# Logits of the next pair but one, two block steps earlier in the second step of a two-step graph attention kernel

## The chip, the cores and the metric

The kernel runs on one core of one Trainium2 chip. The metric is the device time of one execution in microseconds (us). Every duration below comes from one profiled execution of the kernel before, or from the three times shown beside it.

The core has five engines with instruction queues of their own: PE (TensorE, matrix multiplication and transposes), ACT (ScalarE), DVE (VectorE), POOL (GpSimd) and SP (SyncE, which here only issues DMAs). PEld is PE's loading of weights. Each engine works through its queue in order and waits on semaphores that the others raise.

## What is computed

`x` has 3327 rows of 128 numbers and `adj` is 3327 x 3327. Two steps run one after the other; in each, a dense matrix R is applied to one copy of the features and a sparse attention matrix A to the other.

```python
q = X @ W1.T @ W2.T
k = X @ W3.T
logits = q @ k.T / TAU
probs = jax.nn.softmax(logits, axis=-1)
idx = jnp.argsort(-probs, axis=-1)
sp = jnp.take_along_axis(probs, idx, axis=-1)
cs = jnp.cumsum(sp, axis=-1)
keep_sorted = cs - sp < TOP_P                  # TOP_P = 0.9
A = probs * mask                               # mask: the kept ones
A = A / jnp.maximum(A.sum(-1, keepdims=True), 1e-12)
...
R = S + jnp.eye(N); R = R / R.sum(-1, keepdims=True)
for n in range(2):
    A = _top_p_attention(Xa, W1, W2, W3)
    Xf = R @ Xf
    Xa = A @ Xa
    Z = Z + Xf @ U1[n].T + Xa @ U2[n].T
h = X + Z
# layer norm of h with ln_g, ln_b, then layer norm of (x + that)
```

## The kernel before

**Tiles and pairs.** The rows are cut into NT = 26 tiles of 128 (padded to 3328), and two tiles make a pair, so there are NPAIR = 13 pairs, numbered 0 to 12. A row of 3328 columns is cut into NCH = 7 chunks: six of 512 columns and a last one of 256 (255 real ones for logits).

**Units, blocks and bodies.** A unit is the product of one 128-row tile of a matrix with the features: an A unit takes the tile of the attention matrix, an R unit the tile of R. Each unit is seven blocks, one for each chunk. For a block PE transposes four 128 x 128 pieces into a PSUM bank (L602), ACT copies the bank to `blkT` (L721), and two steps later PE multiplies the four pieces with the features (L623). The last chunk has two pieces instead of four. Units are grouped in bodies. In step two, body p holds the two A units of pair p (blocks 0 to 13) and then `STEP_R[p]` R units, four and three in turn (blocks 14 to 41 or 14 to 34). Body p therefore has two steps more than blocks. In step i PE issues, in this order: the transposes of block i, the logits of a chunk if the table `emit` has an entry for i, and the multiplication of block i - 2. ACT issues in step i: the copy of block i, the two copies of a logits chunk if `emit` has an entry, the storing of a finished unit's sums (`part_h`, L742, or `new_x`, L738), parts of the layer norm, and exponentials if the table `exps` has an entry. The last transposes of the A units are in step 13; the sums of the second A unit are stored in step 15.

**Logits.** `logits(s, p, c)` is two matmuls, one for each tile of pair p, with 64 contracted rows (L554). `store_logits` copies both results from PSUM into `E` (L674). `E01` has two areas, and in step two pairs p and p + 2 share one. From body 0 of step two on, there is one PSUM bank for each tile of the pair (bank 0 and bank 1), so that the matmuls of one chunk wait until ACT has copied the chunk before. The lines that set this are:

```python
before = q - (1 if q >= late_logits else 2)          # L545
pe.wait_ge(logits_done, 2 * before + xx + 1)         # L551
if c == 0 and free_at[s, p]:                         # L670, ACT
    act.wait_ge(blk_ready, free_at[s, p])
```

`free_at` is the end of the transposes of the second A unit of pair p - 2, in the same area.

**What a pair needs.** In body p of step two the logits of pair p + 2 are made. DVE takes the eight largest of each run of 32 logits (`v.max`, MAX8, L841), finds the row maximum (`negm`, L866), and ACT makes the exponentials of the pair in step 36 of body p, or steps 36 to 41 where the body has four R units (L691 for the candidates, L696 for the rows). DVE then searches for the threshold of the pair (`search`, from L937 on) and settles it (L1232 to L1261: MATCH_REPLACE8 and the masking), which lets the transposes of that pair's A units start. In its iteration for pair p, DVE searches pair p, takes the maxima of pair p + 1 from some 21 us into the search on (`link.fill = 3`, three MAX8 behind each linked instruction), and then settles pair p. Some pairs also go through `level`, a finer search over the whole rows.

**R tiles.** Two buffers `S` hold two tiles of adj. SP issues the load of R unit n once the transposes of R unit n - 2 are done (L393), and POOL adds the identity (L451) after its work on the sums and the layer norm, in the order of the units; the R unit's first transposes wait for that.

Of the kernel before, what the change touches and what calls it, by code (L numbers as in the profile page):

```python
# [6 lines left out]
def gnn_top_p_kernel(nc, x, adj, W1, W2, W3, U1, U2, ln_g, ln_b, out):  # L7
# [16 lines left out]
    NCH = (NT + CH - 1) // CH  # L24
# [57 lines left out]
    def add_unit(b, kind, s, t):  # L82
        u = Unit()
        u.kind, u.s, u.t, u.k = kind, s, t, len(units)
        u.pair, u.x = t // 2, t % 2
        u.ring, u.accs = (2, ("6",)) if b.early else (3, ("3", "6"))
        if kind == "R":
            u.n, u.src = len(r_units), len(r_units) % 2
            r_units.append(u)
        u.turned = s == 0  # L90
        if u.turned:
            u.j = len(t_units)
            t_units.append(u)
        else:
            u.m = len(units) - len(t_units)
        u.acc = u.accs[u.k % len(u.accs)]
        u.acc_before = acc_user.get(u.acc, -1)
        acc_user[u.acc] = u.k
        u.first = len(seq_unit)
        for c in range(NCH):  # L100
            i = len(seq_unit)
            slot = len(b.seqs) % u.ring
            seq_unit.append(u)
            seq_chunk.append(c)
            seq_slot.append(slot)
            seq_before.append(slot_user.get(slot, -1))
            slot_user[slot] = i
            b.seqs.append(i)
        u.end = len(seq_unit)
        units.append(u)  # L110
        b.units.append(u)

    def new_body(early, s, p, off):
        b = Body()
        b.early, b.s, b.p, b.off = early, s, p, off
        b.units, b.seqs, b.emit, b.exps, b.turn, b.mul, b.first_exps, b.late = [], [], {}, {}, {}, {}, [], {}
        b.look = 1 if early else 2
        bodies.append(b)
        return b

    b = new_body(True, 0, -1, 0)
# [7 lines left out]
    for p in range(NPAIR):  # L129
        more = p + 2 < NPAIR  # L130
        b = new_body(True, 0, p, 0)
# [15 lines left out]
    b = new_body(False, 1, -1, 0)  # L147
# [8 lines left out]
    for p in range(NPAIR):  # L156
        b = new_body(False, 1, p, 0)
        for xx in range(2):
            add_unit(b, "A", 1, 2 * p + xx)
        for n in range(STEP_R[p]):  # L160
            m = len(r_units)
            add_unit(b, "R", m // NT, m % NT)
        if p + 2 < NPAIR:
            for c in range(NCH):
                b.emit[2 * NCH + 2 + c] = (1, p + 2, c)

            for k in range(6):
                b.exps.setdefault(5 * NCH + 1 + (k if STEP_R[p] > 3 else 0), []).append((1, p + 2, k))
# [1207 lines left out]
```

## Time and profile before

| | us |
|---|---|
| three runs | 1434.26, 1433.92, 1429.52 |
| median of the three | 1433.92 |
| profiled execution, its own time | 1431.37 |
| span of its instructions | 1429.3 |
| DVE busy | 1281.5 (90%) |
| PE busy | 1228.1 (86%) |
| ACT busy | 930.7 (65%) |
| POOL busy | 340.5 (24%) |

The time of an execution is its span and some 2.1 us around it. Times in the rows are us from the span's start. Step two's bodies begin at about 525 us (body 0) and the last ends at about 1415 us. The busy shares are means over stages that have different limits, so they don't tell which engine sets the end; the chain of the work that ended last does. In the timeline, one row is a run of like instructions: its start, its length, the engine, the line, and, in brackets, how long the engine sat idle before it and what released it.

### The profile page before, as it was taken

The numbers are of one execution on the slowest core, as the hardware profiler recorded it, in microseconds if no ns is written. First come the engines' busy times: TensorE is split into PE (matmuls) and PEld (weight loads), VectorE is DVE, ScalarE is ACT, GpSimd is POOL, SyncE is SP. The second block draws the span as 40 slices with busy tenths as digits, with TensorE's granted clock in tenths as the row PEclk, the third lists the DMA queues.
The fourth block names the chain that finished last, engine by engine and source line by source line (L and its number), as shares of the span: only waits on it lengthen the run. The fifth ranks groups of instructions, "written<-read, shape, count | busy, mean of one in ns | idle before, by whom it ended". The sixth has DMA issues, their size and how long they took to land.

```text
span 1429.3 us, 29789 instructions
## 1 busy us (share of the span) xinstructions
PE 1228.1 (86%) x9162; PEld 1036.5 (73%) x9162; DVE 1281.5 (90%) x7010; ACT 930.7 (65%) x2026; POOL 340.5 (24%) x584
## 2 busy tenths in 40 slices
PE   7999999999997979897989796919895885929896
PEld 3677777777785968887888786818784775828796
DVE  5998989998976888899989989999998999999995
ACT  5888887788757565756575555636764746646764
POOL 0112322232201331312141220202332222212242
PEclk9999999999998989998999898969998897969998
DMA  5000000000021541412132132211312041211421
GB/s 205 2 1 2 2 2 2 2 2 2 2 97 49 193 145 38 156 49 97 55 139 96 50 103 91 97 48 49 145 50 96 2 145 49 94 52 50 145 49 49
DMA packets 16599, 96.49 MB, mean 68 GB/s; under 512 B 1251, under 2 KB 8930, under 8 KB 9730
## 3 DMA queue, kind: packets, MB, share of 16 engines
q1 hardware_dynamic: 16384, 94.14, 18.7%
q8 instruction: 72, 1.18, 0.3%
q14 instruction: 143, 1.17, 0.3%
HBM read 92.43 MB, written 1.70 MB: 66 GB/s over the span
## 4 chain that ended last, share of the span: by engine, by line
PE 44%; DVE 37%; ACT 11%; issue 5%; POOL 1%; DVEq 1%; DMA 0%; SPq 0%; ACTq 0%; POOLq 0%
PE bank L623 24%; DVE cand L841 13%; PE bank L602 11%; DVE junkC L898 8%; PE bank L554 5%; ACT E L696 4%; DVE E L1241 2%; ACT blkT L721 2%; ACT cand L691 2%; DVE sub L1064 2%; DVE E L1261 1%; PE bank L638 1%; DVE junkS L898 1%; DVE slots L963 1%; ACT S L696 1%
## 5 line engine op out<-in xcount | busy, mean ns | idle before, releaser
L721 ACT ACTIVATE blkT<-bank 128x512 f32<-128x512 f32 (+1 forms) x728 | 406.4, 565 | 284.7 <-PE bank L602 280.7
L841 DVE MAX8 cand<-E 128x8 f32<-128x32 f32 (+1 forms) x2992 | 404.2, 192 | 41.8 <-ACT E L674 26.4
L623 PEld LDWEIGHTS bank<-X,blkT 128*128 128x128 f32 x2704 | 329.1, 191 | 104.1 <-ACT blkT L721 71.8
L623 PE MATMUL bank<-X,blkT 128*128 128x129 f32 (+1 forms) x2704 | 375.9, 281 | 10.3 <-ACT blkT L721 9.1
L602 PE MATMUL bank<-ident,S 128*128 128x128 f32 x1560 | 242.0, 275 | 17.4 <-POOL S L451 15.6
L602 PE MATMUL bank<-ident,E 128*128 128x128 f32 x1144 | 183.0, 285 | 81.0 <-DVE E L1261 81.0
L898 DVE SCALAR_TENSOR_TENSOR junkC<-cand,st 128x128 f32<-128x128 f32 (+2 forms) x390 | 236.0, 613 | 2.0
L623 PE MATMUL bank<-YF,blkT 128*128 128x128 f32 x1352 | 192.7, 287 | 36.1 <-ACT blkT L721 36.1
L623 PEld LDWEIGHTS bank<-YF,blkT 128*128 128x128 f32 x1352 | 171.6, 199 | 68.7 <-ACT blkT L721 57.6
L554 PE MATMUL bank<-kT,Q 64*128 64x512 f32 (+1 forms) x728 | 197.0, 613 | 8.7 <-ACT E L674 8.4
L602 PEld LDWEIGHTS bank<-ident,E 128*128 128x128 f32 x1144 | 143.7, 148 | 83.3 <-DVE E L1261 82.1
L602 PEld LDWEIGHTS bank<-ident,S 128*128 128x128 f32 x1560 | 186.2, 142 | 22.4 <-POOL S L451 17.7
L674 ACT ACTIVATE E<-bank 128x512 f32<-128x512 f32 (+1 forms) x308 | 157.9, 567 | 55.8 <-PE bank L554 55.2
L623 PE MATMUL bank<-YA,blkT 128*128 128x128 f32 x1352 | 187.0, 282 | 0.5 <-ACT blkT L721 0.5
L623 PEld LDWEIGHTS bank<-YA,blkT 128*128 128x128 f32 x1352 | 171.9, 198 | 1.0 <-ACT part_h L742 0.7
L1261 DVE SCALAR_TENSOR_TENSOR E<-E,st 128x3328 f32<-128x3328 f32 x42 | 155.6, 3721 | 8.8 <-DVE flag_i L1041 6.9
L696 ACT ACTIVATE E<-E,negm 128x1664 f32<-128x1664 f32 x88 | 147.4, 1677 | 0.0
L691 ACT ACTIVATE cand<-cand,negm 128x312 f32<-128x312 f32 (+2 forms) x104 | 55.5, 540 | 81.5 <-DVE negm L866 81.5
L480 POOL TENSOR_TENSOR H<-hy,H 128x128 f32<-128x128 f32 x26 | 39.0, 1500 | 281.0 <-ACT hy L757 281.0
L1241 DVE MATCH_REPLACE8 E<-gone,E 128x832 f32<-128x832 f32 x104 | 103.8, 1009 | 0.0
L554 PEld LDWEIGHTS bank<-kT,Q 64*128 64x128 f32 x728 | 56.6, 185 | 43.3 <-issue 27.2
L487 POOL TENSOR_TENSOR H<-part_h,H 128x128 f32<-128x128 f32 x50 | 31.0, 620 | 195.7 <-ACT part_h L742 195.5
(226 smaller groups left out, 1336.6 us busy)
## 6 DMA issues: line engine op xcount, KB each, us to landing
S<-in_adj_dram SPq DMA_DIRECT2D x50, 1663.5 KB, 6.8
S<-in_adj_dram SPq DMA_DIRECT2D x2, 1455.6 KB, 8.5
X<-in_x_dram SPq DMA_DIRECT2D x6, 256.0 KB, 5.4
out_dram<-H SPq DMA_DIRECT2D x1, 1408.0 KB
S<-in_adj_dram SPq DMA_DIRECT2D x2, 194.9 KB, 9.7
u_in<-in_L_gnn_U_dram SPq DMA_DIRECT2D x4, 64.0 KB, 9.6
out_dram<-H SPq DMA_DIRECT2D x1, 128.0 KB
w_in<-in_L_gnn_W_dram SPq DMA_DIRECT2D x2, 32.0 KB, 2.1
```

The lines of the kernel that those rows point to most:

```text
L480: pool.tensor_tensor(H[:, u.t, :], hy[:, z, 0:D], H[:, u.t, :], ALU.add)
L554: pe.matmul(lg_banks(q)[xx][:, 0:LW[c]], Q[h0:h1, p, :], kT[h0:h1, s, c * BANK:c * BANK + LW[c]], start=True, stop=True).then_inc(logits_r ...
L602: m = pe.transpose(BLK[early][slot][:, b * P:(b + 1) * P], src[:, j * P:(j + 1) * P], ident[:, :])
L623: m = pe.matmul(bank[int(u.acc)][:, 0:width], blkT[:, slot, b * P:(b + 1) * P], rhs[:, j, 0:width], start=(j == 0), stop=(j == NT - 1))
L674: act.activation(E[where_e[s, p]][:, xx, c * BANK:c * BANK + LW[c]], lg_banks(q)[xx][:, 0:LW[c]], ACT.Copy).then_inc(logits_done, 1)
L691: act.activation(c, c, ACT.Exp, bias=negm[:, par, xx:xx + 1], scale=1.0, accum_out=total[:, par, xx:xx + 1])
L696: return act.activation(e[:, xx, lo:hi], e[:, xx, lo:hi], ACT.Exp, bias=negm[:, par, xx:xx + 1], scale=1.0, accum_out=Zh[:, par, xx, half: ...
L721: act.activation(blkT[:, slot, 0:w], BLK[early][slot][:, 0:w], ACT.Copy).then_inc(blk_done, 1)
L841: v.max(cand[:, par, xx, 8 * r:8 * r + 8], E[where_e[self.s, self.p]][:, xx, r * w:min((r + 1) * w, N)]).then_inc(s_max, 1)
L898: return v.scalar_tensor_tensor(out=out, in0=a, scalar=limit, in1=a, op0=ALU.is_lt, op1=ALU.mult, accum_out=total)
L1241: link.post(v.match_replace(back, gone[:, xx, k, :], back, 0.0))
L1261: v.scalar_tensor_tensor(out=e[:, xx, :], in0=e[:, xx, :], scalar=one(TSTAR, xx), in1=e[:, xx, :], op0=ALU.is_ge, op1=ALU.mult, accum_out= ...
```

## The change

The seven chunks of the logits of pair p + 2 are issued in steps 14 to 20 of body p in place of steps 16 to 22. That holds for the eleven bodies 0 to 10 of step two, on PE and on ACT. The exponentials stay in step 36. Step one, DVE, POOL and SP have the same instructions in the same order.

```diff
         if p + 2 < NPAIR:
             for c in range(NCH):
-                b.emit[2 * NCH + 2 + c] = (1, p + 2, c)
+                b.emit[2 * NCH + c] = (1, p + 2, c)
 
             for k in range(6):
                 b.exps.setdefault(5 * NCH + 1 + (k if STEP_R[p] > 3 else 0), []).append((1, p + 2, k))
```

PE in body 4, steps 14 to 16, before. The transposes of `S` are those of the first R unit, the multiplications with `YA` the last two of the second A unit, and `kT,Q` are the logits of pair 6:

```order
L602 MATMUL bank5<-ident,S 128x128 x4
L623 MATMUL bank6<-YA,blkT 128x128 x4
L602 MATMUL bank2<-ident,S 128x128 x4
L623 MATMUL bank6<-YA,blkT 128x128 x2
L602 MATMUL bank4<-ident,S 128x128 x4
L554 MATMUL bank0<-kT,Q 128x512
L554 MATMUL bank1<-kT,Q 128x512
L623 MATMUL bank3<-X0,blkT 128x129 x4
```

And in the changed kernel, the same steps:

```order
L602 MATMUL bank5<-ident,S 128x128 x4
L554 MATMUL bank0<-kT,Q 128x512
L554 MATMUL bank1<-kT,Q 128x512
L623 MATMUL bank6<-YA,blkT 128x128 x4
L602 MATMUL bank2<-ident,S 128x128 x4
L554 MATMUL bank0<-kT,Q 128x512
L554 MATMUL bank1<-kT,Q 128x512
L623 MATMUL bank6<-YA,blkT 128x128 x2
L602 MATMUL bank4<-ident,S 128x128 x4
L554 MATMUL bank0<-kT,Q 128x512
L554 MATMUL bank1<-kT,Q 128x512
L623 MATMUL bank3<-X0,blkT 128x129 x4
```

Two chunks of logits have moved ahead, and between the second and the third there now stands the short multiplication (two pieces, `x2`) of the A unit's last block. Before, it stood between transposes alone.

ACT in body 4, steps 14 to 16, before:

```order
L721 ACTIVATE blkT<-bank5 128x512
L721 ACTIVATE blkT<-bank2 128x512
L742 ACTIVATE part_h<-bank6,a_inv 128x128
L721 ACTIVATE blkT<-bank4 128x512
L674 ACTIVATE E01<-bank0 128x512
L674 ACTIVATE E01<-bank1 128x512
```

And in the changed kernel:

```order
L721 ACTIVATE blkT<-bank5 128x512
L674 ACTIVATE E01<-bank0 128x512
L674 ACTIVATE E01<-bank1 128x512
L721 ACTIVATE blkT<-bank2 128x512
L674 ACTIVATE E01<-bank0 128x512
L674 ACTIVATE E01<-bank1 128x512
L742 ACTIVATE part_h<-bank6,a_inv 128x128
L721 ACTIVATE blkT<-bank4 128x512
L674 ACTIVATE E01<-bank0 128x512
L674 ACTIVATE E01<-bank1 128x512
```

The copies of the logits have moved with their matmuls, and the storing of the second A unit's sums now stands between two chunks' copies.

## Rows read from the trace of the kernel before

**Rows 1.** Part 1 of the page: busy time, share of span, instructions.

```profile
PE 1228.1 (86%) x9162; PEld 1036.5 (73%) x9162; DVE 1281.5 (90%) x7010; ACT 930.7 (65%) x2026; POOL 340.5 (24%) x584
```

**Rows 2.** The chain that ended last, merged: start us, length us, engine, tile, line.

```profile
797.32 5.19 ACT E L696 x7
...
823.85 1.11 PE bank L554 x4
844.80 2.52 DVE cand L841 x26
...
1034.94 1.33 ACT E L696
...
1282.00 2.82 PE bank L602 x12
```

**Rows 3.** Waits of DVE from 500 us on: us in total, times, longest.

```profile
DVE st L937 <- ACT E L696: 9.6, 5, 3.7
...
DVE cand L841 <- ACT E L674: 8.1, 5, 2.9
```

**Rows 4.** Timeline of DVE: its first maxima in the iterations of pairs 1 and 5.

```profile
558.66 0.38 DVE L841 MAX8 cand<-E 128x8 f32<-128x32 f32 x3 [2.88 <-ACT E L674]
...
825.63 0.38 DVE L841 MAX8 cand<-E 128x8 f32<-128x32 f32 x3 [2.10 <-ACT E L674]
```

**Rows 5.** Timelines: `negm` on DVE and first exponentials on ACT, bodies 0, 3, 4.

```profile
584.79 0.17 DVE L866 TENSOR_SCALAR negm<-negm 128x2 f32<-128x2 f32 x1
592.11 0.55 ACT L691 ACTIVATE cand<-cand,negm 128x312 f32<-128x312 f32 x1
...
785.83 0.17 DVE L866 TENSOR_SCALAR negm<-negm 128x2 f32<-128x2 f32 x1
792.28 0.55 ACT L691 ACTIVATE cand<-cand,negm 128x312 f32<-128x312 f32 x1
...
869.50 0.55 ACT L691 ACTIVATE cand<-cand,negm 128x312 f32<-128x312 f32 x1 [9.36 <-DVE negm L866]
```

**Rows 6.** Timeline of PE in body 4, steps 14 to 20 (x8 for four pieces).

```profile
821.04 0.60 PE L602 MATMUL bank<-ident,S 128*128 128x128 f32 x4
...
822.80 0.61 PE L623 MATMUL bank<-YA,blkT 128*128 128x128 f32 x4
823.25 0.60 PE L602 MATMUL bank<-ident,S 128*128 128x128 f32 x4
823.78 1.13 PE L554 MATMUL bank<-kT,Q 64*128 64x512 f32 x4
824.84 1.16 PE L623 MATMUL bank<-X,blkT 128*128 128x129 f32 x8
...
826.37 1.13 PE L554 MATMUL bank<-kT,Q 64*128 64x512 f32 x4
...
831.54 1.13 PE L554 MATMUL bank<-kT,Q 64*128 64x512 f32 x4
...
833.90 1.13 PE L554 MATMUL bank<-kT,Q 64*128 64x512 f32 x4
```

**Rows 7.** Timeline of ACT in body 4: copies of the first and the fourth chunk.

```profile
825.00 1.09 ACT L674 ACTIVATE E<-bank 128x512 f32<-128x512 f32 x2 [0.52 <-PE bank L554]
...
832.70 1.08 ACT L674 ACTIVATE E<-bank 128x512 f32<-128x512 f32 x2 [0.46 <-PE bank L554]
```

**Rows 8.** SP and POOL in body 4, third R tile; then the page's DMA row.

```profile
834.00 0.35 SPq L393 DMA_DIRECT2D S<-in_adj_dram  x1
...
845.91 0.46 POOL L451 TENSOR_TENSOR S<-S,ident 128x128 f32<-128x128 f32 x1
...
S<-in_adj_dram SPq DMA_DIRECT2D x50, 1663.5 KB, 6.8
```

**Rows 9.** Busy time by stretch: start:end, length, PE, PEld, DVE, ACT, POOL, PEclk, DMA.

```profile
534.80:555.00 20.20, 19.43 (x147) 19.14 (x148) 19.22 (x73) 8.88 (x19) 3.15 (x4) 0.83 0.00 1
...
738.60:790.20 51.60, 51.39 (x409) 44.87 (x410) 50.19 (x362) 29.96 (x60) 12.23 (x26) 1.00 0.20 73
```

## The prediction

> **What bounds the kernel now.** I read the page's busy times first. DVE at 90% and PE at 86% [rows 1] are both too high for one of them to be the bound everywhere, so the order of the chain is what counts. The chain that ended last [rows 2] is to be read by where it changes engines. Up to 823.85 us step two's chain runs through PE's blocks and ACT's exponentials (such as the piece at 797.32). At 823.85 it passes through two logits matmuls of body 4 and goes over to DVE (844.80), where it stays for most of the next 450 us. It leaves DVE twice: for body 6, whose exponentials end at 1036.3 (the piece at 1034.94), and for good at 1282.00, where PE starts body 10 and PE and ACT set the rest.
>
> So an edit that brings logits forward pays only where DVE both waits for logits and is itself on the chain. DVE's waits [rows 3] give the most that this can be: 8.1 us in 5 waits of DVE for the copies of logits, in all of step two. Two of them are in the timeline [rows 4]: 2.88 us before 558.66, and 2.10 us before 825.63. The other three are 3.1 us together, all before body 4.
>
> Of these, only the one before 825.63 is on the chain. The exponentials of a pair stay in step 36, and ACT reaches that step late: in body 0 `negm` is there at 584.79 + 0.17 = 584.96 and the first exponential starts at 592.11, which is 7.2 us of slack; in body 3 it is 792.28 - 786.00 = 6.3 us [rows 5]. There ACT doesn't wait for DVE, and maxima that come 2 us earlier make the slack longer and nothing else. In body 4 it is the other way round: ACT sat idle for 9.36 us until `negm` came, and its exponentials start at 869.50. What DVE gains before that, everything behind it gains.
>
> **The change part by part.** No instruction is added or taken away. Two chunks of logits stand two steps further up in each of 11 bodies.
>
> *How much earlier the first logits come.* PE's rows of body 4 [rows 6] are to be read as a clockwork. Step 14 begins at 821.04 and step 16 at 823.25, and logits start 823.78 - 823.25 = 0.53 behind the transposes. In the changed kernel they start at 821.04 + 0.53 = 821.57, so 2.21 us earlier than at 823.78. DVE was ready at 825.63 - 2.10 = 823.53. The first copy now ends in time for DVE to go on at 825.63 - 2.21 = 823.42. The wait of 2.10 goes entirely, though by only 0.1 us. Chunks then follow each other at 2.59 us (826.37 - 823.78), and DVE needs about 3 us for the 32 MAX8 of a chunk even without the search's own instructions: its chain piece of 26 takes 2.52 us [rows 2]. So no new wait for a later chunk appears. **Gain: 2.10 us.** What is late next at that point is DVE's own search. I let the gain travel to the end, since from there to 1282 the chain is DVE's, and body 6 itself starts when DVE has settled its pair.
>
> *What the new place costs PE.* The matmuls of one chunk wait until ACT has copied the chunk before. In the fourth pair of matmuls this can be seen closely: they start at 831.54 [rows 6], ACT's copies run from 832.70 to 833.78 [rows 7], and the next ones start at 833.90, 2.36 us after the last and 0.12 behind the copies, in the step whose transposes are two pieces instead of four. I take 2.36 us as the shortest period that the copies allow. In the changed kernel the short multiplication of the A unit's last block stands between the second and the third chunk. It takes 0.45 us (823.25 - 822.80). PE would be ready again after 1.06 (824.84 - 823.78) + 0.45 + 0.53 = 2.04 us, and up to 0.1 later if the short multiplication loses as much behind logits as the long one does. It then waits for 2.36 - 2.04 = 0.32 at most, and 2.36 - 2.14 = 0.22 at least. I take 0.23 us, near the low end, because the long multiplication behind logits is indeed 0.1 longer. A lower bound of nothing is also possible, were the 2.36 PE's own time; an upper bound is 0.32 + 0.37, one store of sums more on ACT, were ACT the late one. Before, this short multiplication had no logits around it, and the last chunk of logits (255 columns) had no successor to wait, so nothing is given back.
>
> This cost counts in the bodies that are on the chain: 0 to 3 in front of 823.85, then 6 and 10. 6 x 0.23 = **1.4 us lost** (0 to 4.1 by the bounds). In the other five bodies PE has idle time to cover it.
>
> *The third R tile.* The load of the R tile for step 28 is issued when the transposes of step 20 are through, at 834.00 in body 4. Six chunks of logits instead of four now precede them, which moves the issue by 2 x (2.59 - 1.33) + 0.23 = 2.75 us (a step without logits takes 1.33: steps 14 and 15 take 2.21, and the short multiplication in them saves 0.45, so (2.21 + 0.45) / 2). The load takes 6.8 us, so it lands at 834.00 + 2.75 + 6.8 = 843.6. POOL takes that tile at 845.91 [rows 8], behind its own work. The load stays hidden by 2.3 us, and costs nothing; without that cover, each us of it would be a us of PE in that body. DVE, POOL and SP pass no new instruction, and the norm's work on ACT and POOL in steps 18 and 25 stands in the same steps as the R tiles that wait for it.
>
> *The area in `E`.* The copies need the end of the A unit's transposes, step 13, and ACT's own block copy of step 14 comes behind that. The edit is at the earliest place that needs no new wait.
>
> **Sum.** -2.10 + 1.4 = -0.7 us. Against the profiled execution, 1431.37, that is 1430.7; against the median of the runs, 1433.92, it is 1433.2. The four executions have a mean of 1432.3, and less 0.7 that is 1431.6. I forecast **1432.0 us**, no change that can be measured. About 0.5%, 7 us, is what a measurement of this kernel can tell from none.
>
> One rule of the Trainium skill speaks against the change (Perfetto Trace Analysis, Optimizing Tensor Performance, Matmuls): independent groups of matmuls should rotate through PSUM banks, so that the emptying of one overlaps the next. The logits here have one bank per tile, and the 2.36 us period agrees with the rule; by it the crowded place is the short multiplication, and the sum holds it already.
>
> **Rivals.**
>
> *All of DVE's waits count* (chance 0.04). Then 8.1 us less what the earlier start can give: 1431.4 - 8.1 = 1423 us. It would need DVE to be the bound in bodies 0 to 3. The 6.3 and 7.2 us of slack before the exponentials [rows 5] speak against it.
>
> *PE loses more than DVE gains* (chance 0.15). The place is step 16 of bodies 0 to 3, 6 and 10, the price the upper bound above, 0.69 us each: 4.1 - 2.1 = +2.0, so 1434 us, slower, but not measurably. It decides from 0.35 us per body on. For it speaks that ACT has the sums' store as well between the second and the third chunk; against it, that ACT is idle for 0.46 us before the copies of a chunk [rows 7].
>
> *The granted clock falls in the denser steps* (chance 0.03). In the stretch 534.8 to 555.0 the granted clock is 0.83, that is, (1 - 0.83) / 0.5 x 20.2 = 6.9 us at 1.2 GHz and the rest at 2.4 GHz, right behind a stretch in which PE stood waiting for ACT [rows 9]. Another such piece in each of six bodies would cost 6 x 6.9 / 2 = 21 us: 1452 us. Against it: in body 3, with seven chunks of logits in the same tight alternation, the clock was 1.00 throughout. By the Trainium skill (TensorE: Matmul & The Clock Gate, A second HAM failure mode: psum-queue depth-cycling), frequent short idling between groups that cycle through PSUM can drop the clock; body 3 doesn't bear that out.
>
> *The logits don't come earlier at all* (chance 0.03), because something that I read as free holds ACT: only the cost is left, 1431.4 + 1.4 = 1432.8.
>
> **How the numbers follow.** Forecast 0.75, rivals 0.04, 0.15, 0.03, 0.03. The likeliest case gives 1432.0. The low end is the lowest execution shown less the whole gain, 1429.5 - 2.1 = 1427.4; the high end the highest plus the second rival's loss, 1434.3 + 2.0 = 1436.3. That holds all but the first and third rival, and some of what executions scatter. Faster by over 0.5%: 0.04, the first rival. Slower by over 0.5%: 0.04, the third and a little scatter. The rest, 0.92, is within 0.5%.
>
> **What would show it.** Right: DVE's wait before its first maxima of pair 6 is gone, and so are most of those of pairs 2 and 4; the slack before the exponentials in bodies 0 and 3 grows by about 2 us; from the end of the exponentials in body 3 (797.32 + 5.19 = 802.5 on the chain) to the exponentials of body 4 (869.50) it takes 65 us in place of 67; PE's third logits of a body start 2.36 us behind the second. Wrong: exponentials in bodies 0 to 3 that start before their old time relative to the body, which would make DVE the bound there; a wait of PE for POOL or a DMA at step 28 that is longer than before; a clock below 1.00 in bodies 1 or 3.

## The result

| | us | runs |
|---|---|---|
| before, median | 1431.68 | 9 (1428.89 to 1434.26) |
| changed, median | 1438.26 | 9 (1435.09 to 1441.62) |
| profiled execution before, span | 1429.3 | |
| profiled execution changed, span | 1435.0 | |

The changed kernel is slower: the ratio is 1.0046, with a 95% interval of 1.0033 to 1.006, that is 6.6 us. The forecast was 1432.0 us with a range of 1427.4 to 1436.3. The time lies outside the range, and what was to be no measurable change is a small loss, of 4.7 to 8.6 us by the interval. Here and below, the ratio is an estimate over all the runs with an interval of its own; it isn't exactly the quotient of the two medians.

### The profile page after: what moved, and what is told of

Same layout as the page of the kernel before. It is cut to its first block, busy times and chain, and to the rows that moved or that the text cites. A ratio compares the mean times of both kernels' runs of the same rounds, so it can differ in the third digit from the quotient of the medians.

```text
span 1435.0 us, 29789 instructions
## 1 busy us (share of the span) xinstructions
PE 1230.9 (86%) x9162; PEld 1039.0 (72%) x9162; DVE 1280.8 (89%) x7010; ACT 929.1 (65%) x2026; POOL 353.3 (25%) x584
## 4 chain that ended last, share of the span: by engine, by line
DVE 42%; PE 39%; ACT 10%; issue 6%; POOL 2%; DVEq 1%; DMA 0%; SPq 0%; ACTq 0%; POOLq 0%
PE bank L623 21%; DVE cand L841 15%; PE bank L602 10%; DVE junkC L898 9%; PE bank L554 5%; ACT E L696 4%; DVE E L1241 3%; ACT blkT L721 2%; ACT cand L691 2%; DVE E L1261 2%; DVE sub L1064 2%; DVE slots L963 1%; PE bank L638 1%; DVE st L908 1%; DVE junkS L898 1%
## 5 line engine op out<-in xcount | busy, mean ns | idle before, releaser
L1261 DVE SCALAR_TENSOR_TENSOR E<-E,st 128x3328 f32<-128x3328 f32 x42 | 156.0, 3730 | 8.8 <-DVE flag_i L1041 6.9
```

Source lines behind the costliest of these rows:

```text
L1261: v.scalar_tensor_tensor(out=e[:, xx, :], in0=e[:, xx, :], scalar=one(TSTAR, xx), in1=e[:, xx, :], op0=ALU.is_ge, op1=ALU.mult, accum_out= ...
```

## The profile after

Part 1 of the changed kernel's page, to be read against [rows 1]:

```profile
PE 1230.9 (86%) x9162; PEld 1039.0 (72%) x9162; DVE 1280.8 (89%) x7010; ACT 929.1 (65%) x2026; POOL 353.3 (25%) x584
```

PE, DVE and ACT have the busy time that they had, within 3 us. POOL has the same 584 instructions and is busy for 353.3 us; before it was 340.5. Nothing in the edit touches POOL, so some of its instructions must have become longer. The chain that ended last shows where, as against [rows 2]:

```profile
587.34 3.81 POOL S L451
...
722.73 4.03 POOL YF L477
...
848.86 3.63 DVE cand L841 x38
```

Two single POOL instructions of about 4 us each are now on the chain, one in body 0 and one in body 2. Before, no piece of POOL stood on it between the start of body 0 and body 4. These two account for 6.8 of POOL's 12.8 us more; most of the rest are two small instructions, L464 and L463, which take 3.58 and 3.36 us at 595.01 and 730.77, and for which nobody waits. The timelines of POOL, DVE and PE around the first of them, in the changed kernel:

```profile
586.74 0.60 POOL L477 TENSOR_SCALAR YF<-hy,row_inv 128x128 f32<-128x128 f32 x1
587.30 3.83 POOL L451 TENSOR_TENSOR S<-S,ident 128x128 f32<-128x128 f32 x1
...
587.14 3.69 DVE L1261 SCALAR_TENSOR_TENSOR E<-E,st 128x3328 f32<-128x3328 f32 x1
...
591.19 0.66 PE L602 MATMUL bank<-ident,S 128*128 128x128 f32 x4 [2.40 <-POOL S L451]
```

and the same place before:

```profile
588.14 0.46 POOL L451 TENSOR_TENSOR S<-S,ident 128x128 f32<-128x128 f32 x1
...
588.42 0.08 DVE L1241 MATCH_VALUE_LOAD E<-gone,E 128x8 f32 x1
588.49 1.01 DVE L1241 MATCH_REPLACE8 E<-gone,E 128x832 f32<-128x832 f32 x1
...
589.53 3.68 DVE L1261 SCALAR_TENSOR_TENSOR E<-E,st 128x3328 f32<-128x3328 f32 x1
...
589.46 0.60 PE L602 MATMUL bank<-ident,S 128*128 128x128 f32 x4
```

Before, POOL adds the identity for the R tile of step 35 in 0.46 us, beside DVE's MATCH_REPLACE8, and DVE's masking (L1261) starts 0.9 us behind it. Now the masking starts 2.4 us earlier, just ahead of POOL's instruction. POOL's 0.46 us become 3.83 us, and it ends 0.3 us behind the masking: 587.30 + 3.83 = 591.13 against 587.14 + 3.69 = 590.83. PE stands still for 2.40 us. In body 2 it is L477, the instruction ahead of the addition, that is met; it takes 4.05 us in place of 0.60. PE waits as long there:

```profile
722.71 4.05 POOL L477 TENSOR_SCALAR YF<-hy,row_inv 128x128 f32<-128x128 f32 x1
...
722.68 3.69 DVE L1261 SCALAR_TENSOR_TENSOR E<-E,st 128x3328 f32<-128x3328 f32 x1
...
727.23 0.66 PE L602 MATMUL bank<-ident,S 128*128 128x128 f32 x4 [2.47 <-POOL S L451]
```

The wait that DVE has lost comes back as a wait of DVE for ACT's exponentials, as against [rows 3]:

```profile
DVE st L937 <- ACT E L696: 20.5, 5, 8.4
DVE cand L841 <- issue: 8.9, 3, 4.5
```

The five waits for the copies of logits (8.1 us) are gone altogether. The waits for exponentials went from 9.6 to 20.5 us; behind bodies 0 and 2 they are 7.9 and 8.4 us in place of 3.7 and 3.5, and there ACT is late by PE's wait as well.

Why bodies 0 and 2 and not 1 and 3? The waits for logits that the change takes away were not alike. [Rows 4] show those of bodies 0 and 4, 2.88 and 2.10 us. The ones of bodies 1 and 2, before:

```profile
626.08 0.38 DVE L841 MAX8 cand<-E 128x8 f32<-128x32 f32 x3 [0.18 <-ACT E L674]
...
692.52 0.38 DVE L841 MAX8 cand<-E 128x8 f32<-128x32 f32 x3 [2.74 <-ACT E L674]
```

In bodies 1 and 3 DVE waited for logits for 0.18 and 0.19 us only, so its later instructions hardly moved there.

The other rows of the prediction have their answers too. PE's clockwork in body 4, as against [rows 6]:

```profile
825.87 1.13 PE L554 MATMUL bank<-kT,Q 64*128 64x512 f32 x4
...
828.45 1.13 PE L554 MATMUL bank<-kT,Q 64*128 64x512 f32 x4
...
830.59 1.28 PE L554 MATMUL bank<-kT,Q 64*128 64x512 f32 x4
...
833.33 1.13 PE L554 MATMUL bank<-kT,Q 64*128 64x512 f32 x4
```

The third chunk's matmuls start 2.14 us behind the second's and the fourth's 2.74 behind those, 4.88 in all. The delay is seen inside the third chunk, whose matmuls take 1.28 us in place of 1.13; the profile doesn't name what held them. Without it the distance would be some 2.13 + 2.59 = 4.72 (2.13 is the prediction's 2.04 and most of the 0.1 it allowed), so PE loses 0.16 us per body. ACT's copies of the second chunk:

```profile
829.61 1.09 ACT L674 ACTIVATE E<-bank 128x512 f32<-128x512 f32 x2 [0.46 <-PE bank L554]
```

They end at 829.61 + 1.09 = 830.70, and the third chunk's matmuls have started at 830.59: the tile that goes first has a bank of its own, and needs only the first of the two copies.

Then DVE's maxima behind a branch in the iteration of pair 5, as the timeline of DVE has them: before, then changed, with SP's issue of the load of adj in the changed kernel between them:

```profile
844.80 0.29 DVE L841 MAX8 cand<-E 128x8 f32<-128x32 f32 x2 [1.72 <-issue]
```

```profile
840.97 0.35 SPq L393 DMA_DIRECT2D S<-in_adj_dram  x1
...
848.86 0.29 DVE L841 MAX8 cand<-E 128x8 f32<-128x32 f32 x2 [3.41 <-issue]
```

This is a wait for nothing that the profile shows, right behind a branch. It grew by 1.7 us. The load of adj was issued at 834.00 before [rows 8], 9.1 us ahead of the start of this wait; now it is issued 4.5 us ahead of it and is under way when DVE comes to the branch, as a load takes 6.8 us.

## The experiments

The theory after this reading is **A**: the early logits free DVE, its masking moves onto POOL's work for the R tile of step 35 in bodies 0 and 2, and PE waits. The rivals are **B**, the matmuls of the logits wait for ACT's copies, and **C**, the loss lies behind body 4. All times stand beside runs of the kernel before on the same chip. The diffs are against the kernel before, unless it is said otherwise.

### Only bodies 0 and 2, and all but these

```diff
-                b.emit[2 * NCH + 2 + c] = (1, p + 2, c)
+                b.emit[2 * NCH + (0 if p in (0, 2) else 2) + c] = (1, p + 2, c)
```

> Only bodies 0 and 2 of step two have their logits two steps earlier. Theory A (collision): DVE, freed of its wait for logits, starts the masking instruction L1261 (3.7 us, two operands from SBUF) some 2.4 us earlier, onto POOL's addition of the identity for the R tile of step 35; POOL's instruction then lasts 3.8 us in place of 0.46 and PE waits 2.4 us for it. Two bodies: 2 x (2.4 + 0.16) = 5.1 us slower than before, with a wait of PE for L451 of about 2.4 us at step 35 of bodies 0 and 2. Theory B (the matmuls of the logits wait for ACT, 0.16 us per body as the changed kernel's trace has it): +0.3 us. Theory C (the loss comes from behind body 4: code loading and body 10): +0.3 us.

Measured: 1439.81 us against 1431.16, ratio 1.0052 (1.0038 to 1.0065).

```diff
-                b.emit[2 * NCH + 2 + c] = (1, p + 2, c)
+                b.emit[2 * NCH + (0 if p not in (0, 2) else 2) + c] = (1, p + 2, c)
```

> All bodies but 0 and 2 have their logits two steps earlier. Theory A: what is left of the changed kernel's +6.6 us without the two collisions, so +1 to +2 us over before. Theory B: +5 us (9 of 11 bodies). Theory C: +6 us.

Measured: 1431.11 us against 1431.16, ratio 0.9998 (0.9988 to 1.0007).

The whole loss sits in two of the eleven bodies. B and C fall as its cause: on the second kernel they had put +5 and +6 us, and it is at -0.3 us (-1.7 to +1.0). Theory A has the place right, but neither of its sums: it had +1 to +2 us for the second kernel, and the first lost 7.4 us (5.4 to 9.3), more than the 5.1 us that I had added up. The first kernel's timeline of body 0, POOL and PE, and the busy time of a stretch behind it:

```profile
588.59 4.05 POOL L477 TENSOR_SCALAR YF<-hy,row_inv 128x128 f32<-128x128 f32 x1
...
593.12 0.71 PE L602 MATMUL bank<-ident,S 128*128 128x128 f32 x4 [2.47 <-POOL S L451]
```

```profile
594.00:598.00 4.00, 4.00 (x25) 4.00 (x24) 3.96 (x6) 1.76 (x5) 0.35 (x1) 0.62 0.37 155
```

Right behind the wait the granted clock over 4 us is 0.62, so most of that stretch ran at 1.2 GHz: (1 - 0.62) / 0.5 x 4 = 3.0 us of it, of which half, 1.5 us, is lost. In the changed kernel's own trace the granted clock was 1.00 behind both waits (590 to 594 and 727 to 731 us). Three profiled executions, the changed kernel's, this one and that of the early logits with POOL's new order (further down), have six of these waits at step 35 of bodies 0 and 2. Two were followed by such a fall, this one and the one of body 2 in the last of the three (0.58 over 727.8 to 731.8 us). So a collision costs 2.2 to 2.5 us and, in some executions, some 1.5 us more. By the Trainium skill (TensorE: Matmul & The Clock Gate, Part 1: The HAM clock gate) the clock falls when PE has been idle; that agrees with this row, though not every wait of this length brought it about.

### DVE held back, everything else as changed

In the changed kernel (against which this diff is), DVE's first maxima in the iterations of pairs 1 and 3 wait for the second chunk of logits in place of the first:

```diff
-                            dve.wait_ge(logits_done, 2 * lg_seq(self.s, self.p, c) + xx + 1)
+                            first = 1 if self.n == 0 and self.s and self.p in (2, 4) else 0
+                            dve.wait_ge(logits_done, 2 * lg_seq(self.s, self.p, c + first) + xx + 1)
```

> The changed kernel, but in the iterations of pairs 1 and 3 DVE waits for the second chunk of the next pair's logits before its first maximum, which puts its maxima and the masking behind them back to about where they stood before (0.7 us earlier at most). PE, ACT and POOL have the changed kernel's order. Theory A: POOL's L451 for step 35 of bodies 0 and 2 lasts 0.46 us again, PE doesn't wait for it, and the kernel is 4.8 us faster than the changed one, so +1 to +2 us over before. Theories B and C: as slow as the changed kernel, +6.6 us, since PE's order is what it was there.

Measured: 1432.57 us against 1431.16, ratio 1.0003 (0.9993 to 1.0013). A wait was added to the busiest engine and the kernel became some 6 us faster than the changed one, where 4.8 were expected. POOL and DVE in body 0:

```profile
589.32 0.46 POOL L451 TENSOR_TENSOR S<-S,ident 128x128 f32<-128x128 f32 x1
...
591.41 3.68 DVE L1262 SCALAR_TENSOR_TENSOR E<-E,st 128x3328 f32<-128x3328 f32 x1
```

The addition takes 0.46 us again, and PE doesn't wait for it. PE's order is that of the changed kernel, so B falls a second time.

### The masking in four pieces

The changed kernel again (the diff is against it), with L1261 cut in the iterations of pairs 1 and 3; the sums of the pieces are added behind it:

```diff
+                            if s and p in (1, 3):
+                                for k in range(MATCH):
+                                    piece = e[:, xx, k * MW:(k + 1) * MW]
+                                    ins = v.scalar_tensor_tensor(out=piece, in0=piece, scalar=one(TSTAR, xx), in1=piece,
+                                                                 op0=ALU.is_ge, op1=ALU.mult, accum_out=part[:, xx, k:k + 1])
...
```

> The changed kernel, but in the iterations of pairs 1 and 3 the masking L1261 is four instructions of 832 columns (about 0.95 us each) in place of one of 3328. Theory A in the form that POOL's instruction waits for the end of the DVE instruction that it meets: POOL's L451 lasts at most 1.4 us, PE's wait at step 35 falls below 0.5 us, and the kernel is about 4 us faster than the changed one (+2 to +3 over before). If POOL is kept out for the whole of the masking, however it is cut, the wait stays at 2.4 us and the time at +6.6 us.

Measured: 1432.90 us against 1431.16, ratio 1.0008 (0.9999 to 1.0018). POOL, DVE and PE in body 0:

```profile
587.89 1.43 POOL L477 TENSOR_SCALAR YF<-hy,row_inv 128x128 f32<-128x128 f32 x1
589.29 0.98 POOL L451 TENSOR_TENSOR S<-S,ident 128x128 f32<-128x128 f32 x1
...
587.76 1.08 DVE L1264 SCALAR_TENSOR_TENSOR E<-E,st 128x832 f32<-128x832 f32 x1
588.77 1.18 DVE L1264 SCALAR_TENSOR_TENSOR E<-E,st 128x832 f32<-128x832 f32 x1
...
590.33 0.66 PE L602 MATMUL bank<-ident,S 128*128 128x128 f32 x4 [0.39 <-POOL S L451]
```

The overlap is still there, at the same moment, but POOL gets its turn when a piece ends: 1.43 and 0.98 us in place of 4.05 or 3.83, and PE waits 0.39 us. So POOL waits for the end of the DVE instruction that it meets, not for the end of the masking. Only body 0 of this trace tests that. In body 2 POOL's addition had begun 0.23 us before the first piece, and it wasn't held up:

```profile
722.43 0.46 POOL L451 TENSOR_TENSOR S<-S,ident 128x128 f32<-128x128 f32 x1
...
722.66 1.12 DVE L1264 SCALAR_TENSOR_TENSOR E<-E,st 128x832 f32<-128x832 f32 x1
```

### One step earlier in place of two

```diff
-                b.emit[2 * NCH + 2 + c] = (1, p + 2, c)
+                b.emit[2 * NCH + 1 + c] = (1, p + 2, c)
```

> All logits one step earlier, steps 15 to 21. Before, DVE's masking L1261 begins some 0.95 us behind the end of POOL's L451 for step 35 of body 0. Step 15 is 0.88 us long, so DVE's wait shrinks by 0.88, and PE and POOL come 0.16 later: the two then begin within 0.1 us of each other. If the addition is met, L451 lasts 3.8 us in one or both of bodies 0 and 2, in some executions at least, and the time is up to 5 us over before; if it just escapes, the time is that of before within 1 us. The theory doesn't tell which; it tells that no third value comes, and that the time goes with that row.

Measured: 1429.84 us against 1431.24, ratio 0.9998 (0.9986 to 1.0011).

```profile
587.90 0.46 POOL L451 TENSOR_TENSOR S<-S,ident 128x128 f32<-128x128 f32 x1
...
588.75 3.69 DVE L1261 SCALAR_TENSOR_TENSOR E<-E,st 128x3328 f32<-128x3328 f32 x1
```

The masking comes 0.4 us behind the end of the addition, not onto it, and the time is that of before. My figure of 0.1 us for the distance was off, but the time went with the row as said. One step is clear of the collision here and two aren't.

### Only body 4, and the same with a short load

```diff
-                b.emit[2 * NCH + 2 + c] = (1, p + 2, c)
+                b.emit[2 * NCH + (0 if p == 4 else 2) + c] = (1, p + 2, c)
```

> Only body 4 of step two has its logits two steps earlier: the one place where DVE's wait for logits (2.10 us) is on the chain. If the gain were all that happens there, 2.1 us faster than before. By the trace of the changed kernel, the load of the third R tile, now 2.75 us later, meets the loading of DVE's code behind its branch, and DVE's wait after the branch grows from 1.7 to 3.4 us; then 1 us at most is left, no difference that can be measured. No wait of PE for POOL at step 35 of bodies 0 and 2.

Measured: 1432.05 us against 1432.55, ratio 0.9998 (0.9988 to 1.0007).

On top of this, one load is cut short. The kernel then leaves out most of one tile of R, so it only serves to measure:

```diff
+                elif u.n == 26:
+                    sp.dma_start(S[0:16, u.src, 0:N], adj[r0:r0 + 16, :]).then_inc(adj_loaded[u.src], 16)
```

> As only_4, but the adj load of R unit 26 (for step 28 of body 4) brings 16 rows in place of 128; the other rows of that buffer keep an older tile, so that part of R is left out. If the load is what delays DVE's code, DVE's wait before its maxima after the branch in the iteration of pair 5 is 1.7 us or less instead of 3 or more, and the time is 1 to 2 us below only_4. If the code's lateness has another cause, the wait stays above 2.8 us.

Measured: 1428.80 us against 1432.55, ratio 0.9982 (0.997 to 0.9995). The wait behind the branch, first in the kernel with body 4 alone, then with the short load:

```profile
844.61 3.76 DVE L841 MAX8 cand<-E 128x8 f32<-128x32 f32 x38 [3.23 <-issue]
```

```profile
842.90 3.63 DVE L843 MAX8 cand<-E 128x8 f32<-128x32 f32 x38 [1.72 <-issue]
```

With the load cut from 128 rows to 16 the wait is 1.72 us, exactly that of before, and the gain forecast for this place appears: 2.6 us by the ratio (0.7 to 4.3), where the forecast had 2.1. The place itself shows it more closely. From the end of body 3's exponentials (802.5 us in both) to the first of body 4 it takes 64.8 us with the short load, against 67.0 before [rows 5]:

```profile
867.37 0.55 ACT L693 ACTIVATE cand<-cand,negm 128x312 f32<-128x312 f32 x1 [7.91 <-DVE negm L868]
```

With the full load 1.5 of the 2.1 us are lost behind the branch. The other traces agree at this place. Where the load was issued 7.3 to 9.1 us ahead of the wait (before, bodies 0 and 2 alone, one step earlier, and POOL's new order with the logits as before) the wait was 1.71 or 1.72 us; in the seven with the full load issued 4.5 to 5.0 us ahead of it, it was 2.85 to 3.41 us. That DVE's code is what comes late is an inference: in the trace, packets of the kind "instruction" lie there (three of one queue in the 8 us around it, before and with body 4 alone), and the profile names no releaser.

### POOL's addition ahead of its norm work

This one was made to beat both kernels. PE's waits for L451 at steps 28 and 35 of bodies 6 and 10, on the chain, were there before the change. POOL reaches the addition only behind the round of the layer norm, which itself waits for ACT. Here it adds the identity first:

```diff
                 elif u.k <= last_part.k:
                     add_part(u)
+                    next_diagonal(units[u.k + 1])
                     for job in norm_rounds.get(u.k + 1, ()):
                         norm_round(*job)
```

`next_diagonal` is the two `add_diagonal` conditions that stood at the head of the loop, where it is called too, each done once.

> Logits as before. POOL adds the identity to the R tile of the next unit but one before its part of the layer norm, not behind it. If PE's waits for L451 at steps 21, 28 and 35 are POOL's order alone, they go: in bodies 6 and 10, which are on the chain, 1.2 + 2.0 us each, and 1.7 in body 11, of which the tile's load may keep 1.6. 5 to 7 us faster than before. If the loads set those waits, no difference.

Measured: 1428.31 us against 1432.55, ratio 0.9972 (0.9958 to 0.9985). That is 4.0 us faster (2.1 to 6.0), a little less than the 5 to 7 expected. PE's waits for POOL's addition in step two, first before, then with POOL's new order:

```profile
PE bank L602 <- POOL S L451: 15.6, 11, 2.8
```

```profile
PE bank L611 <- POOL S L451: 2.8, 3, 1.4
```

Of the 12.8 us that PE waits less, those in the two bodies on the chain count: from the first transposes of one body to those of the next, body 6 takes 70.3 us in place of 72.7 and body 10 takes 70.1 in place of 71.8, 4.1 us together.

> pool_first with the changed kernel's logits, two steps earlier in all bodies. The collisions of bodies 0 and 2 are between POOL's saving of sums (L475 to L477, L451) and DVE's masking, which this order of POOL doesn't touch: there the identity is added behind the saving as before. So PE's waits of some 2.4 us at step 35 of bodies 0 and 2 stay, and the kernel is 5 us or more slower than pool_first. If putting POOL's addition first cured the collision too, it would be equal to pool_first.

Measured: 1434.34 us against 1432.55, ratio 1.001 (0.9999 to 1.0021), 6.0 us slower than its twin with the logits in their old place by the medians, 5.4 by the ratios. POOL and PE in body 0:

```profile
588.18 3.87 POOL L451 TENSOR_TENSOR S<-S,ident 128x128 f32<-128x128 f32 x1
...
592.11 0.66 PE L611 MATMUL bank<-ident,S 128*128 128x128 f32 x4 [2.44 <-POOL S L451]
```

The collision costs as much in another surrounding, within the noise, which is the comparison of before and changed made a second time.

> POOL's addition ahead of its norm work, as in pool_first, and the logits two steps earlier in all bodies but 0 and 2. With the logits moved but not in 0 and 2 the time was that of before, so this should be equal to pool_first: 1428 us, no difference between the two. Faster than pool_first by 1 us or more would mean that the early logits gain something once PE doesn't wait for POOL.

Measured: 1426.27 us against 1431.24, ratio 0.9969 (0.9958 to 0.9979). It is the fastest kernel here by its ratio, but it can't be told from `pool_first` (0.9972): as expected, the early logits of the other bodies bring nothing that can be measured.

## Why the prediction was wrong, point by point

**What bounds the kernel, and where the gain is: right.** Only DVE's wait before 825.63 was on the chain, and it went entirely. With the load out of the way the gain was seen at that size, 2.2 us in the trace and 2.6 (0.7 to 4.3) in the time.

**"Maxima that come 2 us earlier make the slack longer and nothing else": this step failed**, and the forecast with it. The sum has no term for a wait of PE for POOL; it put that at nothing. The slack before the exponentials did grow: in body 0 from 7.2 to 11.3 us, part of it because PE and ACT came later. In body 3, for which about 2 us were forecast too, it grew by 0.4 us only, since DVE had hardly waited for logits there. But slack only says that nobody waits for the result. Where DVE's instructions then lie in time changes too, and here a 3.7 us instruction moved onto a 0.46 us instruction of POOL that PE does wait for. Two collisions at 2.4 us are 4.9 us, with PE's 0.16 us for each 5.1. That lies within the interval of the 6.6 us. The rest of the 6.6 fits the fall of the clock behind some of these waits; how often it comes in the runs without a profile isn't known. In bodies 1 and 3 nothing was met: from the end of one body's exponentials to the end of the next's they took 64.07 and 64.06 us in place of 63.90 and 63.92, which is the 0.16 us of the crowded step and nothing more. The prediction had named a longer wait of PE for POOL as a sign of being wrong, but at step 28; it came at step 35.

**"DVE, POOL and SP pass no new instruction": true and not enough.** I checked the order on each queue and the waits on semaphores. The meeting of two engines is neither. By the Trainium skill (GPSIMD Engine Reference, Specifications) POOL shares its SBUF interfaces with DVE, and they contend when the DVE instruction has two inputs from SBUF. The traces agree: L451 lasts 3.83 us beside L1261, whose two tensor operands are both `E`. Beside MATCH_REPLACE8 it lasts 0.46 us; that row names `gone` and `E`, but in front of it stands a MATCH_VALUE_LOAD of 8 numbers for the first. No run has the masking with one operand, so that the second operand is what matters rests on the page. The trace of before held the warning, just ahead of body 0. There the same addition takes 3.59 us beside L1261:

```profile
521.54 3.59 POOL L451 TENSOR_TENSOR S<-S,ident 128x128 f32<-128x128 f32 x1
...
521.07 3.75 DVE L1261 SCALAR_TENSOR_TENSOR E<-E,st 128x3328 f32<-128x3328 f32 x1
```

I weighed other rules in its place.

**"I let the gain travel to the end": too simple.** In the changed kernel 1.7 of the 2.1 us were gone 20 us later, behind DVE's branch, since the load of adj moved as well. The prediction had moved that load by 2.75 us, about rightly (2.6 measured from the end of body 3's exponentials), and asked only whether POOL would wait for it. Who else uses the DMA engines in the new place was not asked.

**PE's cost for the crowded step: near in size, by luck.** 0.23 us forecast, 0.16 measured, per body. But 2.36 us is not the shortest period that the copies allow: the third chunk started 2.14 us behind the second, where 2.36 was named as the sign of being right, and ahead of the end of both copies. What makes up the 0.16 us inside the chunk isn't shown.

**The rivals.** The second had the right sign, with the wrong place and price: its own step cost the 0.16 us. The first and the fourth didn't come. The third, the clock, came as a consequence of PE's new wait, not of the denser steps: in the changed kernel's trace the granted clock was 1.00 through bodies 1 and 3 (605 to 656.6 and 742 to 795 us).

**What the two traces can't be used for.** Their spans differ by 5.7 us, close to the 6.6, but partly for other reasons. Body 0, by the ends of the exponentials, is only 1.3 us longer in the changed kernel's: behind its start the granted clock is 0.91 over 20.2 us, where it was 0.83 before [rows 9], and that gives back (0.91 - 0.83) / 0.5 x 20.2 / 2 = 1.6 us. Body 10 took 74.7 us from its first transposes to those of body 11, against 71.8 before. It also took 74.8 us in the kernel with all bodies but 0 and 2, whose time is that of before, and 72.3 with DVE held back, where it has the early logits too. Most of it is the clock. In both traces PE waits 2.01 us for POOL's addition at step 35 of body 10; the 5 us behind that, before and changed:

```profile
1337.60:1342.60 5.00, 4.97 (x45) 4.97 (x46) 4.86 (x15) 3.54 (x10) 0.46 (x1) 1.00 0.57 238
```

```profile
1341.10:1346.10 5.00, 5.00 (x31) 5.00 (x32) 4.90 (x11) 1.95 (x6) 0.41 (x1) 0.66 0.56 235
```

That is (1 - 0.66) / 0.5 x 5 / 2 = 1.7 us. In the first 6 us of the body the granted clock is 0.52 in place of 0.69, another 1.0 us. Together they are 2.7 of the 2.9 us.

**Open.** What decides whether the clock falls behind such a wait, since the same wait of 2.01 us was followed by 1.00 in one trace and by 0.66 in the other.

## What to carry to other kernels

An engine with slack isn't free to move: before bringing its work forward, lay its long instructions over the other engines' short ones at the new time, above all DVE instructions with two SBUF operands over POOL's, and the DMAs over what else is being loaded. If an engine's busy time has grown with the same instructions, look for the few that became several times longer. Where such a collision can't be avoided by timing, cut the long instruction into pieces. Putting the short one that somebody waits for ahead in its queue is worth trying for its own sake: it made 4.0 us here, but it didn't cure the collision.

## What the runs showed of the hardware

- A POOL instruction that began just behind a DVE `scalar_tensor_tensor` with two SBUF operands waited for its end: 0.46 us became 3.83, and 0.60 became 4.05. With pieces of about 1.1 us they became 0.98 and 1.43. An addition that began 0.23 us ahead of such a piece took its 0.46 us, as it did beside MATCH_REPLACE8.
- At one place, DVE's first instruction behind a branch waited 1.71 or 1.72 us when no load of adj was under way (four traces), and 2.85 to 3.41 us when one of 1.66 MB was (seven traces); with a load of an eighth of the rows it was 1.72 us.
- After PE had stood for 2.47 us the granted clock was 0.62 over 4 us that followed, after 2.16 us it was 0.58 over 4 us, and after 2.01 us it was 0.66 over 5 us; behind waits of 2.40, 2.47 and 2.01 us in other places or executions it was 1.00.
